# Attention and expert network on one core: the slots' products by one level of Strassen's scheme

## The reference

```
xn = layernorm(x)
q, k, v = xn @ Wq.T + bq, xn @ Wk.T + bk, xn @ Wv.T + bv
phi = elu(.) + 1;  kv_sum = cumsum(phi(k) * v) along the sequence
s = (phi(q) * kv_sum * SCALE) @ Wo.T + bo
# router: 8 experts, top 2, 256 places each; all experts share w1 and w2
h = gelu(xn @ w1.T + b1) @ w2.T + b2
g = silu(h * sum of the router weights of the kept choices)
out = x + s * g
```

## Time and profile before

| | us |
|---|---|
| median of 3 runs | 2227.52 (2223.86 to 2227.53) |
| span of the profiled execution | 2223.5 |
| PE busy | 2163.5 (97%) |
| DVE busy | 993.6 (45%) |
| ACT busy | 464.5 (21%) |
| POOL busy | 117.6 (5%) |
| slots' stage, first to last matmul | 532.0 to 2200.2 |

### The profile page before, as it was taken

How to read it: one execution, slowest core, us unless ns; L and a number is a source line. 1 busy time by engine, 2 the same in 40 slices (tenths; PEclk the granted TensorE clock), 3 DMA queues, 4 the chain that set the end, 5 groups by cost and what they waited for, 6 DMA issues and landing times.

```text
span 2223.5 us, 27700 instructions
## 1 busy us (share of the span) xinstructions
PE 2163.5 (97%) x10228; PEld 991.7 (45%) x10228; DVE 993.6 (45%) x1657; ACT 464.5 (21%) x692; POOL 117.6 (5%) x158
## 2 busy tenths in 40 slices
PE   8699999998999999999999999999999999999995
PEld 2245554554444444444444444444444444444442
DVE  3666665664544545334433433433433433433444
ACT  1232222222312222111111111111111111111132
POOL 1000000002600002000000000000000000000013
PEclk9899999999999999999999999999999999999998
DMA  8521111112311224110110110110110110110048
GB/s 308 194 86 38 45 50 38 57 38 66 84 46 38 70 81 165 57 38 21 54 38 26 49 38 28 47 38 28 47 42 24 47 46 20 47 66 19 10 113 189
DMA packets 53545, 140.92 MB, mean 63 GB/s; under 512 B 6096, under 2 KB 26640, under 8 KB 52240
## 3 DMA queue, kind: packets, MB, share of 16 engines
q1 hardware_dynamic: 47840, 123.27, 17.3%
q0 software_dynamic: 5680, 17.36, 3.2%
HBM read 113.32 MB, written 44.09 MB: 71 GB/s over the span
## 4 chain that ended last, share of the span: by engine, by line
PE 93%; DMA 3%; DVE 2%; issue 1%; SPq 0%; ACT 0%; POOL 0%; DVEq 0%; ACTq 0%; POOLq 0%
PE pair L1145 37%; PE pair L1130 36%; PE pair L1077 16%; PE pair L1009 2%; PE pair L1050 1%; DMA arena_b<-x_t 1%; PE pair L1086 1%; DMA kvs_dram<-arena_b 0%; DVE arena_a L677 0%; DMA out<-arena_b,meta_s 0%; PE pair L1018 0%; DMA stage<-w_groups 0%; DMA arena_b<-s_dram 0%; DMA arena_b<-x 0%; DVE arena_b L878 0%
## 5 line engine op out<-in xcount | busy, mean ns | idle before, releaser
L1145 PE MATMUL pair<-arena_b 128*128 128x512 f16 x3840 | 842.3, 380 | 5.2 <-DVE arena_b L920 5.2
L1130 PE MATMUL pair<-xnT,arena_b 128*128 128x512 f16 x3840 | 843.2, 380 | 3.0 <-DVE arena_b L878 3.0
L1145 PEld LDWEIGHTS pair<-arena_b 128*128 128x128 f16 x3840 | 376.1, 98 | 460.1 <-issue 8.5
L1130 PEld LDWEIGHTS pair<-xnT,arena_b 128*128 128x128 f16 x3840 | 376.4, 98 | 458.2 <-issue 7.1
L928 DVE SCALAR_TENSOR_TENSOR arena_a<-pair,arena_a 128x512 f32<-128x512 f32 x640 | 423.1, 686 | 160.2 <-PE pair L1145 156.5
L920 DVE SCALAR_TENSOR_TENSOR arena_b<-arena_b 128x512 f16<-128x512 f32 x160 | 105.3, 691 | 672.2 <-ACT arena_b L605 672.0
L1077 PE MATMUL pair<-arena_a,arena_b 128*128 128x512 f16 x1728 | 383.6, 380 | 3.8 <-DVE xnT L282 3.8
L596 ACT ACTIVATE arena_b<-pair,b_c 128x512 f32<-128x512 f32 x128 | 87.9, 687 | 912.0 <-PE pair L1130 911.9
L1077 PEld LDWEIGHTS pair<-arena_a,arena_b 128*128 128x128 f16 x1728 | 169.3, 98 | 197.7 <-issue 6.6
L878 DVE SCALAR_TENSOR_TENSOR arena_b<-stage,arena_b 128x1024 f16<-128x1024 f32 x80 | 97.7, 1223 | 29.7 <-ACT arena_b L566 29.6
L605 ACT ACTIVATE arena_b<-arena_b 128x512 f16<-128x512 f32 x160 | 92.9, 621 | 24.8 <-DVE arena_b L915 24.8
(11 more groups left out here) (143 smaller groups left out, 683.7 us busy)
## 6 DMA issues: line engine op xcount, KB each, us to landing
stage<-w_groups SPq DMA_DIRECT2D x80, 512.0 KB, 4.0
arena_b<-x_t SPq DMA_DIRECT2D x8, 2048.0 KB, 8.2
arena_b<-x SPq DMA_DIRECT2D x20, 512.0 KB, 4.5
kvs_dram<-arena_b SPq DMA_DIRECT2D x20, 512.0 KB, 3.5
arena_b<-kvs_dram SPq DMA_DIRECT2D x32, 256.0 KB, 2.6
s_dram<-arena_a POOLq DMA_DIRECT2D x4, 2048.0 KB, 7.0
arena_b<-s_dram SPq DMA_DIRECT2D x16, 512.0 KB, 5.0
arena_b<-w_kv SPq DMA_DIRECT2D x8, 512.0 KB, 5.4
```

The lines of the kernel that those rows point to most:

```text
L1130: ins = mm(out_bank(FT * (j % 2) + f), w[:, a, c % 4, f * P:(f + 1) * P], xnT[:, b, c, (j % BLOCKS) * BLOCK:(j % BLOCKS + 1) * BLOCK], sta ...
L1145: ins = mm(out_bank(4 + m % 4), h_hl[j % 2][:, f, a, (m // 2) * P:(m // 2 + 1) * P], ring[par][:, 2 + f, b, (m % 2) * BLOCK:(m % 2 + 1) * ...
```

## The change

Up and down products of the slots' stage are made in blocks by Strassen's scheme in Winograd's form: a product of 2 x 2 blocks takes 7 block products where the plain one takes 8. One operand is summed into S1 to S4, the other into T1 to T4, and the results are sums of the products P1 to P7.

**Units.** The slots are taken in two halves of 1024 (`HALVES`), each in two blocks of 512. The groups now have 512 hidden columns (`GROUPS` = 10: 2 of q and O, 8 of the network) and two quads each. A *quad* makes 2 x 2 blocks: 256 hidden columns for 1024 slots, 7 products of 12 matmuls over 4 of the 8 chunks of channels. Its values are named 11, 12, 21, 22. A *down* makes 2 x 2 blocks of output from a group's two quads: 7 products of 4 tiles x 6 matmuls. Quads are numbered k = 0 to 39, downs n = 0 to 19; PE runs quad 0, quad 1, and then for each n quad 2n+2, down n, quad 2n+3; the first half ends with quad 19 and down 9, and the second begins with quad 20.

**Sums of x.** Before the first quad PE adds and subtracts the blocks of `xnT` with `ident` and `nident` (112 matmuls, L1688), ACT and DVE split the results. Those of the second half of slots go to `xop_dram`, with its raw blocks, and are read back ahead of quad 20.

**A quad.** P1, P6, P5 and P3 add up in one bank of PSUM. ACT copies that bank out before the next product is added (`keep_product`), and DVE adds the other products (`c11`, `p167`, `c22`, `c21`). ACT and DVE then make the values as before, the DVE sums them to S3, S2, S4, S1, and both split seven operands (`high_g`, `low_g`) where there were four.

**Weights.** In the first half SP loads raw blocks, POOL forms the sums (`sums_up`, `sums_up_late`, and in `down` T3, T2, T4, T1). ACT makes high halves. The low halves are made by DVE for quads (`low_up`), by POOL for downs (`low_down`) and for quad 0. SP saves each split operand to `up_dram` or `down_dram`. In the second half SP loads these, and nothing of a weight is computed.

**Around it.** DVE's first add of a block starts `acc`, with b_2 in it for the network, in place of POOL's copies. b_o is added by POOL to the rows of s (`bias_s`). `acc` holds one half of the slots (32 KB). Gates and scatters of the first half follow down 9, its tiles 4 to 7 within quad 20; those of the second half stand behind down 19. The q operand loads are issued by ACT. The loops are written out.

The core of the diff:

```diff
-GF = 256
+GF = 512
+HALVES = 2
+UP = (1, 2, 6, 7, 5, 4, 3)
+DOWN = (2, 1, 6, 5, 3, 7, 4)
+A_OF = {1: "11", 2: "12", 3: "S4", 4: "22", 5: "S1", 6: "S2", 7: "S3"}
+B_OF = {1: "11", 2: "21", 3: "22", 4: "T4", 5: "T1", 6: "T2", 7: "T3"}
...
+            def product(k, j, out_to, first):
+                pe.wait_ge(up_w[j], 16 * (k + 1))
+                if k == 2 * GROUPS:
+                    pe.wait_ge(x_loaded[j], 32)
+                x_in_op, w = x_op(B_OF[UP[j]]), up_ring(j)
+                i = 0
+                for c in range(4):
+                    for a, b in PASSES:
+                        ins = mm(out_to, w[:, a, c * P:(c + 1) * P], x_in_op[:, b, c, :],
+                                 start=(first and i == 0), stop=(i == 11), skip_group_check=True)
+                        i += 1
+                ins.then_inc(up_done, 1)
...
+            def down(n):
+                for j in range(7):
+                    name = DOWN_A[j]
+                    pe.wait_ge(down_w[j], 16 * (n + 1))
+                    pe.wait_ge(g_lo, made_count(2 * n + 1, name))
+                    for t in range(PAIRS):
+                        h, e = t // 2, 14 * n + 2 * j + t // 2
+                        if t % 2 == 0 and e >= 2:
+                            pe.wait_ge(down_added, e - 1)
...
+            def low_down(n, j):
+                name = B_OF[DOWN[j]]
+                pool.wait_ge(down_hi, 7 * n + j + 1)
+                nc.gpsimd.tensor_tensor(down_ring[:, j, :, LO, :], w_pair(name), down_ring[:, j, :, HI, :],
+                                        ALU.subtract).then_inc(down_w[j], 16)
...
+                low_down(n, 0)
+                pool.wait_ge(down_scaled, 4 * n + 4)
+                nc.gpsimd.tensor_tensor(w_pair("T3"), w_pair("22"), w_pair("12"), ALU.subtract).then_inc(down_sum, 1)
+                low_down(n, 1)
...
+            load_up(k0 + 1)
+            for i in range(4, HALF_TILES):
+                sp.wait_ge(fin_stored[i - 4], 16)
+                load_s(0, (i,))
...
+                p167(k)
+                if half and k == 2 * GROUPS:
+                    for i in range(PAIRS, HALF_TILES):
+                        result(0, i)
```

1062 lines of the change are left out of this document (776 added, 286 removed).

## The result

The changed kernel takes **2236.39 us** (2233.41 to 2237.70) where the kernel before takes 2225.89 on the same chip: ratio 1.0047, 95% interval 1.0033 to 1.0061. I had forecast 2183, so the sign is wrong: 0.5% slower, not 2% faster. The profiled span is 2231.7 us against 2223.5. A second comparison gave 1.0035 (1.0017 to 1.0054); on another chip, where the kernel before takes 2245.9, the ratio is 0.997 (0.9959 to 0.9981). Two executions, one of each kernel, took 4934 and 9410 us; they are left out of every time and ratio here.

A forecast was written before the change was run, and what follows sets the result against it. PE, 97% busy with matmuls, was taken as the bound. Savings of 183.0 us and the other terms summed to -44.5: 2223.5 to 2179.0, plus 4.0 around the span, 2183 us; range 2100 to 2270, the forecast's own 2150 to 2215.

The forecast's parts named there:

- 848 matmuls fewer, old stage's waits gone: Slots' stage: 848 fewer matmuls at 0.2158 us save 183.0 us; the old stage's 10.6 us of waits go too.
- sums of x: Start of stage: ACT's DMA issues, weight wait and scaling, DVE's work and saves of x delay quad 0; +13 us (8 to 22).
- attention quads: 8 of 40 quads: late last values and ACT's P1 copy hold PE, about 4 us at 3 places, 2 at 3; +18 us.
- downs of the first half: First-half downs: PE waits for POOL's weight work and port-delayed adds, 6.0 x 9, plus 8 in the last; +62 us.
- boundary: Between halves: PE stands in quad 21 while four results wait for late loads and go tile by tile; +32 us (22 to 38).
- clock: After waits of about 5 us PE's next matmuls run slower, 2.3 us each time; +12 us (4 to 40).
- end: Behind the last matmul: eight results and scatters in one burst, 3.5 us each, 36.6 against 23.3; +13 us (7 to 20).
- each port wait is up to 2.1; much falls into PE's wait for POOL, and I add 0.8: First-half downs: DVE's adds, with about 1.0 us of room, are delayed by POOL at the port; 0.8 us per down.
- The term of 5.2 from POOL's chain: First-half downs: POOL's seven units end at D + 20.7, where product 3 wants its weight at D + 15.5; 5.2 us.
- (1): POOL's two-input sums as fast as a copy, 1.04 us, or DVE's bursts keep the port: 2117 us; chance 0.28.
- (2): First-half downs: POOL retakes the port after each DVE instruction, 19 us per down instead of 6: 2300 us; chance 0.16.
- (3): Short PE waits in most quads and downs lower the clock, 40 places at 2.3 us: 2257 us; chance 0.08.

## Why the prediction was wrong, point by point

In the order of the forecast's sum (us; forecast, then measured in the profiled run):

| term | forecast | measured |
|---|---|---|
| 848 matmuls fewer, old stage's waits gone | -193.6 | -193.6: the second half runs at the old pitch |
| start of the stage | -0.9 | +1.4 |
| sums of x | +13 | +17.9 |
| attention quads | +18 | +25.0 (21.0 in quads 0 to 4, 4.0 in quads 23 to 26) |
| other quads of the first half | 0 | +2.4 |
| downs of the first half | +62 | +86.1 |
| boundary | +32 | +43.6 (41.2 and down 10's 2.4) |
| clock | +12 | 28, in the other rows |
| last down | 0 | +16.1 |
| end | +13 | +9.2 |
| sum | -44.5 | +8.1; the span says +8.2 |
| median above the profiled span | 4.0 | 4.7 |

- **Downs of the first half: the step that failed is "each port wait is up to 2.1; much falls into PE's wait for POOL, and I add 0.8".** The term of 5.2 from POOL's chain isn't in the changed kernel at all, where PE never waits for a low half. It is there once DVE's sums stand apart, with 3.6 us (0.38 and 3.20). The overlap was the mistake: the port waits do not fall into that wait. They come earlier in the down, at products 1 and 2, through three held instructions in a row ahead of an add with 1.4 us of room (2.59 for half a product, less 1.22 for the add). Their time is spent before the chain's is due, and it pushes the down to 44.2 on average. The units were mis-sized in part. A low half takes 2.12 us where DVE doesn't compete, my 2.1, and 2.25 on average; a sum takes 2.35 and up to 2.80. The Trainium skill (GPSIMD Engine Reference, Performance versus the Vector engine) led to an estimated 2.3 for a sum; the trace agrees, with 2.35 us.
- **Down 0** was priced like the others and cost 13.2: its start has four DVE instructions of the attention contexts as well, three of them held (1.43, 2.50 and 2.82 us), ahead of L1394 and L1398 at 2.59 and 2.71.
- **The last down: the second step that failed, a term not in the sum at all.** I saw the eight instructions ahead of the first add, gave them 8 us in down 9, and forgot that down 19 has the same code, with POOL's biases of 2.65 us each beside it. Three of the eight run alone and take 0.69 us; the other five are held and take 13.9. Taking them apart gave 12.6 back.
- **Boundary**: one hole ended in the right place and by the mechanism named, 34.30 us, with each tile's round 6.05 us (1441.79 to 1447.84) and not 5.2: the bias takes 2.90 here, and starts only when the scatter is issued. That the rest is the attention chain's is argued, not shown.
- **Sums of x**: PE's wait is the one named, but longer, since ACT's six issues take 12.69 us of its queue (0.5 to 4.6 each), which I had counted as nothing.
- **End**: eight scatters at 1.85 to 2.27 us apart are faster than the 3.5 that I took.
- **FFN quads**: forecast with no wait, and nearly so: 36.6 for a pair, 0.3 above the ideal. With ACT's copy of P1 earlier it is 36.3.
- **Rivals.** (1) is dead: 2.12 at the least, not 1.04. (2) has the right mechanism, POOL back on the port after every DVE instruction, at 8.0 us a down and not 19, since POOL stands for ACT in between and DVE meets it five times, not fifteen. My sign for it, two-input instructions above 1.5 us on average, would have missed it: the means are 1.0 to 1.1. Alone it would have left a gain, as its point was 11 us; without the last down's 16.1 beside it, the kernel would still be ahead. The Trainium skill (SBUF — State Buffer, Who interferes with whom) speaks of a lock held for a whole instruction; the ends 0.54 us apart agree. (3), the clock, is there in part: in down 4 the lot of 60 matmuls behind the 3.60 us took 14.81 us, with a granted clock of 0.56 from 998.90 to 1002.40; in down 3 behind the same wait it took 13.12. The first half was granted 0.97. In the whole stage 136 matmuls, each at about 0.42 us behind the one before and not 0.2158, cost 28 us, where I had 12.
- **The range**, 2100 to 2270, held the time, since it took in both ends of the port's cost; the forecast's own, 2150 to 2215, did not. Its likeliest case added up what single stages lose and gave each the value nearer to nothing.

The change does what it says and its price was about its gain. Which of the two is larger depends, at 0.3 to 0.5%, on the chip.

## What to carry to other kernels

Where POOL and DVE both read SBUF in a steady loop, count every DVE instruction with two SBUF inputs as long as one of POOL's and a little more (2.5 to 2.8 us here), and avoid two in a row ahead of one that PE waits for. When two chains are late by nearly the same time, easing either gains little (8 and 13 us of the downs' time here, 50 with both and POOL's low halves moved): look for the next limit before judging a fix by its own gain. A mean over a whole kernel can hide a few long instructions in the place that counts. A code path that runs in the steady state and again at the end has to be priced in both places.

## What the runs showed of the hardware that I had not expected

- POOL and DVE take turns at the port, one instruction each, for as long as both want it: four DVE instructions in a row took 2.77 us each (11.07 for L1412 x4 at 2153.45) beside POOL's biases. POOL pays as well: its sums take 2.35 us where it doesn't stand behind DVE and up to 2.80 where the two take turns.
- A memset on POOL, also one of 1.80 us, doesn't hold DVE's two-input instructions at all (688 ns beside 0.69 alone).
- Six DMA issues of 512 KB in a row on ACT's queue took 12.69 us of it, and 12.40 on SP's.
- The kernel before is 0.8% slower on some chips (2243 to 2246 us for 2226), the changed kernel is not (2236 to 2238 on either).
